# A position matrix added on TensorE, an earlier row maximum, expert choice on logits, and beta added once

## What is computed

```python
prod2 = lhs2 @ rhs2                                  # per batch: 256 x 256, inner size 16
S = softmax(V_s @ sigmoid(prod2 + b_s), axis=1)      # b_s: the position matrix, 256 x 256
out = sum over k of (cheb[k] * S).T @ x, times Theta[k]
y = relu(rw @ x + conv(relu(out)) + biases)
x = x + (y - mean(y)) / sqrt(var(y) + 1e-5) * gamma + beta     # over the 16 times
xn = groupnorm(x)
probs = softmax(xn_tokens @ gate_w.T); rw, sel = top_k(probs, 2); rw = rw / rw.sum()
x = x + sum over the two chosen experts of rw * expert(xn_token)
```

## Time and profile before

| | us |
|---|---|
| median of 3 runs (lowest, highest) | 695.96 (695.71, 696.68) |
| the profiled execution, its own time | 695.89 |
| its span in the trace | 694.1 |
| PE busy over the span | 556.2 (80%) |
| DVE busy | 402.7 (58%) |
| ACT busy | 242.3 (35%) |
| POOL busy | 217.3 (31%) |
| mean granted clock of PE | 0.904 of full |

### The profile page before, as it was taken

How to read it: one execution, slowest core, us unless ns; L and a number is a source line. 1 busy time by engine, 2 the same in 40 slices (tenths; PEclk the granted TensorE clock), 3 DMA queues, 4 the chain that set the end, 5 groups by cost and what they waited for, 6 DMA issues and landing times. The chain is left out here.

```text
span 694.1 us, 11673 instructions
## 1 busy us (share of the span) xinstructions
PE 556.2 (80%) x2488; PEld 363.4 (52%) x2489; DVE 402.7 (58%) x1793; ACT 242.3 (35%) x603; POOL 217.3 (31%) x283
## 2 busy tenths in 40 slices
PE   0567599999999999999982408999999999998243
PEld 0233357766666666766661203666666666665122
DVE  4645226788888888888898552333333333332355
ACT  0343144344444444444431201333333333333232
POOL 5000001224444444444455430344334333434000
PEclk9989599999999999999996556999999999999555
DMA  9900000000000000000000142222222222220796
GB/s 306 415 3 1 1 0 1 0 1 32 31 32 32 31 31 32 32 30 32 32 31 31 49 105 56 90 85 83 81 89 86 83 83 90 89 84 28 219 300 207
DMA packets 36259, 52.84 MB, mean 76 GB/s; under 512 B 4605, under 2 KB 31360, under 8 KB 35968
## 3 DMA queue, kind: packets, MB, share of 16 engines
q1 hardware_dynamic: 24816, 30.86, 14.2%
q0 software_dynamic: 6480, 16.85, 6.6%
q10 hardware_dynamic: 4928, 4.72, 2.1%
HBM read 30.19 MB, written 23.14 MB: 77 GB/s over the span
## 5 line engine op out<-in xcount | busy, mean ns | idle before, releaser
L610 PE MATMUL bank<-w,xT 128*128 x284 | 137.6, 608 | 2.1 <-DVE xT L1399 2.1
L1399 DVE COPY xT<-bank 128x256 f32<-128x256 f32 x71 | 30.2, 425 | 146.9 <-PE bank L597 146.9
L960 POOL DMA_INDIRECT yrows<-xT,dest x71 | 69.4, 977 | 141.4 <-ACT xT L816 135.2
L929 POOL DMA_INDIRECT xrows<-xtok,slot x64 | 67.9, 1061 | 82.1 <-DVEq L1296 67.5
L487 PE MATMUL bank<-work 128*128 128x256 f32 x384 | 93.3, 386 | 0.0
L917 POOL TENSOR_TENSOR yg<-work,sml 128x512 f32<-128x512 f32 x16 | 17.9, 1122 | 187.3 <-DVE work L1206 187.3
L487 PEld LDWEIGHTS bank<-work 128*128 128x128 f32 x384 | 70.4, 190 | 9.0 <-issue 0.8
L625 PE MATMUL bank<-w,xT 128*128 x284 | 73.3, 381 | 1.6 <-ACT xT L821 1.6
L610 PEld LDWEIGHTS bank<-w,xT 128*128 128x128 f32 x284 | 49.3, 194 | 38.2 <-issue 38.2
L810 ACT ACTIVATE xT<-bank 128x256 f32<-128x256 f32 x71 | 27.2, 383 | 98.5 <-PE bank L610 98.5
L625 PEld LDWEIGHTS bank<-w,xT 128*128 128x128 f32 x284 | 48.5, 190 | 6.2 <-issue 2.6
(11 more groups left out here) (201 smaller groups left out, 1020.1 us busy)
## 6 DMA issues: line engine op xcount, KB each, us to landing
xT<-xrows SPq DMA_DIRECT2D x71, 129.0 KB, 2.1
xT<-yrows SPq DMA_DIRECT2D x32, 256.0 KB, 3.9
xs<-x_in SPq DMA_DIRECT2D x4, 1024.0 KB, 11.1
w<-w13t_in SPq DMA_DIRECT2D x1, 4096.0 KB, 18.0
out<-xT ACTq DMA_DIRECT2D x16, 256.0 KB, 3.8
w<-w2t_in SPq DMA_DIRECT2D x1, 2048.0 KB, 22.3
yrows<-xT,dest POOLq DMA_INDIRECT x71, 2.4
xrows<-xtok,slot POOLq DMA_INDIRECT x64, 2.8
```

What stands on the lines that cost most here:

```text
L610: last = mm(bank[2 + q][:, :], xc[:, q, c], w13[:, e, c].rearrange("p w n -> p (w n)"), start=(c == 0), stop=(c == C - 1))
L929: pool.indirect_dma_start(xrows, bass.IndirectOffsetOnAxis(ap=slot[:, q, w, k:k + 1], axis=0), xtok[:, q, k], None).then_inc(sc_done[q], 16)
L960: pool.indirect_dma_start(yrows, bass.IndirectOffsetOnAxis(ap=dest[:, q], axis=0), yo[:, q], None, bounds_check=2 * TOKENS - 1, oob_is_err ...
L1399: V.tensor_copy(xc[:, q].rearrange("p c k -> p (c k)"), bank[q][:, 0:C * P]).then_inc(c_xc, 1)
```

## The change

Six edits, made together:

1. **Position matrix on PE.** Before, DVE added `bs` to the position product and wrote `sg`. Now one product of the identity with `bs`, 512 columns wide, starts PSUM bank 1, the two position products accumulate onto it, and ACT's tanh reads the bank.
2. **Row maximum earlier.** On DVE the softmax part is given to `weave` together with the layer norm's first part, so the row maximum stands right behind the relu of y. ACT takes `exps` ahead of `square`, and tanh ahead of `normalise`.
3. **Choice on logits.** The expert choice compares the logits less their maximum, where it compared softmax probabilities. The first expert has difference 0. ACT takes the exponential of one value per token (2 columns) where it took 16 columns. The two weights 1/(1+e) and e/(1+e) are worked out in `route_c`.
4. **Splits.** `features` uses rows 0 to 63 and 64 to 127 of the array in separate products of 192 columns, into banks 4 and 5. The gate product is split into two token halves of 128 columns that land on partitions 0 and 64. One transpose of 72 rows replaces the two of 8 rows.
5. **Beta once.** POOL no longer adds beta for each batch. ACT adds it to all of `xs` in the prologue, with 16 instructions, one for each time t: 512 elements for each partition, 64 bytes apart, in place. Eight stand ahead of the second group's tanh, four ahead of its exponential, four behind.
6. POOL waits for those 16 ahead of its first turn.

```diff
             def product(b, p):
                 pe.wait_ge(s["b_lr"], done(b))
                 pe.wait_ge(s["b_exp"], done(b - 1))
+                mm(bank[1][:, :], ident, bs[:].rearrange("p c n -> p (c n)"), start=True, stop=False, skip_group_check=True)
                 for c in range(C):
                     last = mm(bank[1][:, c * N:(c + 1) * N], lr[0:T, p, N + c * P:N + (c + 1) * P],
-                              lr[0:T, p, 0:N], start=True, stop=True)
+                              lr[0:T, p, 0:N], start=False, stop=True, skip_group_check=True)
...
             def features(b, p, c):
 
+                pe.wait_ge(s["b_zc"], (b * 4 + c * 2) + START)
                 for h in range(H):
-                    pe.wait_ge(s["b_zc"], (b * 4 + (c * H + h)) + (START - 1))
-                    mm(bank[4 + h][:, 0:K * P], xT[:, b, h, c * P:(c + 1) * P],
-                       thetabd[:].rearrange("p k t o -> p (k t o)"), start=True, stop=True).then_inc(s["b_z"], 1)
+                    for r in range(2):
+                        rows = slice(r * P // 2, (r + 1) * P // 2)
+                        last = mm(bank[4 + r][:, h * K * P // 2:(h + 1) * K * P // 2], xT[rows, b, h, c * P:(c + 1) * P],
+                                  thetabd[rows, :, r * TH // 2:(r + 1) * TH // 2].rearrange("p k t o -> p k (t o)"),
+                                  start=True, stop=True)
...
                 for c in range(C):
-                    last = mm(bank[3][0:E, 0:FT], sm("gate")[:, c * E:(c + 1) * E], xn2[:, c], start=(c == 0),
-                              stop=(c == C - 1))
+                    for k in range(TT):
+                        last = mm(bank[3][64 * k:64 * k + E, 0:P], sm("gate")[:, c * E:(c + 1) * E],
+                                  xn2[:, c, k * P:(k + 1) * P], start=(c == 0), stop=(c == C - 1))
...
+            def add_beta(first, end):
+
+                act.wait_ge(a_xnv, B)
+                act.wait_ge(a_xna, B)
+                for t in range(first, end):
+                    nc.scalar.activation(x_all[:, :, :, t], x_all[:, :, :, t], ACT.Identity,
+                                         bias=sm("beta")[:, t:t + 1], scale=1.0).then_inc(x_beta, 1)
+
...
             normalise_and_copy(1, 6, GB + 2)
+            add_beta(0, T // 2)
             temporal_tanh(1)
+            add_beta(T // 2, 3 * T // 4)
             temporal_exp(1)
+            add_beta(3 * T // 4, T)
...
             def tanh(b, p):
-                act.wait_ge(s["b_bs"], done(b))
-                nc.scalar.activation(sg[:, p], sg[:, p], ACT.Tanh, scale=0.5).then_inc(s["b_th"], 1)
+                act.wait_ge(s["b_pr"], done(b))
+                act.wait_ge(s["b_L"], done(b - 2))
+                nc.scalar.activation(sg[:, p].rearrange("p c n -> p (c n)"), bank[1][:, :], ACT.Tanh, scale=0.5).then_inc(s["b_th"], 1)
...
                 step(nc.gpsimd.tensor_tensor(flat(yg[:]), flat(y[:, p]), over(sm("gamma")), ALU.mult))
-                step(nc.gpsimd.tensor_tensor(flat(yg[:]), flat(yg[:]), over(sm("beta")), ALU.add))
...
-            def add_bs(b, p):
-                dve.wait_ge(s["b_pr"], done(b))
-                dve.wait_ge(s["b_L"], done(b - 2))
-                V.tensor_tensor(sg[:, p].rearrange("p c n -> p (c n)"), bank[1][:, :],
-                                bs[:].rearrange("p c n -> p (c n)"), ALU.add).then_inc(s["b_bs"], 1)
-                yield
-
...
-                weave(centre())
-                weave(router(route_a), statistics())
-                variance = layer_norm()
-                weave(attention(), along=(variance, choice))
-                weave(variance, group_norm(), matrices(), choice)
+                weave(centre(), attention(), router(route_a), statistics())
+                weave(layer_norm(), group_norm(), matrices(), choice)
                 weave(router(route_c))
```

More of the change, by code:

```diff
@@ L534, in turn_logits @@
                 pe.nop(nofuse=True)
-                for k in range(TT):
-                    last = nc.tensor.transpose(bank[3][:, FT + k * E:FT + (k + 1) * E], lgT[0:E, k * P:(k + 1) * P],
-                                               cst[0:E, ID:ID + E])
-                last.then_inc(s["b_lg"], 1)
+                nc.tensor.transpose(bank[3][:, FT:FT + 64 + E], lgT[0:64 + E], cst[0:64 + E, ID:ID + 64 + E]
+                                    ).then_inc(s["b_lg"], 1)
             def prefix(b, p):
@@ L745, in copy_features @@
             def copy_features(b, p, c):
-                for h in range(H):
-                    act.wait_ge(s["b_z"], (b * 4 + (c * H + h + 1)) + START)
-                    nc.scalar.copy(z[:, p, c, :, h], bank[4 + h][:, 0:K * P].rearrange("p (k o) -> p k o", k=K)
+                for r in range(2):
+                    act.wait_ge(s["b_z"], (b * 4 + (c * 2 + r + 1)) + START)
+                    nc.scalar.copy(z[:, p, c, :, :, r * P // 2:(r + 1) * P // 2],
+                                   bank[4 + r][:, 0:K * P].rearrange("p (h k o) -> p k h o", h=H, k=K)
                                    ).then_inc(s["b_zc"], 1)
@@ L977, in _ @@
             V = nc.vector
-            for n in "b_bs b_max b_rec b_A b_y b_cen b_var b_dn b_st b_q b_nb b_sh b_M b_slot".split():
+            for n in "b_max b_rec b_A b_y b_cen b_var b_dn b_st b_q b_nb b_sh b_df b_M b_slot".split():
                 dve.sem_inc(s[n], START)
@@ new lines, in route_b @@
+                step = Steps(dve, v_rt2, b, 10)
+                yield from step.then(V.scalar_tensor_tensor(out=rt[:, 4], in0=rt[:, 0], scalar=0.0, in1=row8(cs(DSC, E)),
+                                                            op0=ALU.is_equal, op1=ALU.mult))
+                yield from step.then(V.tensor_reduce(r2[:, 5], rt[:, 4], AX, ALU.max))
+                yield from step.then(V.tensor_tensor(rt[:, 7], rt[:, 4], wide8(r2[:, 5]), ALU.is_equal))
+                yield from step.then(V.scalar_tensor_tensor(out=rt[:, 5], in0=rt[:, 7], scalar=-3e38, in1=rt[:, 0],
+                                                            op0=ALU.mult, op1=ALU.add))
@@ new lines, in route_b @@
+                yield from step.then(V.tensor_reduce(r2[:, 4], rt[:, 5], AX, ALU.max))
+                dve.sem_inc(s["b_df"], 1)
+                V.tensor_scalar(xtok[:, p, :, N + 1], r2[:, 5], -1.0, float(E), ALU.mult, ALU.add)
+                yield from step.then(V.tensor_tensor(rt[:, 3], rt[:, 5], wide8(r2[:, 4]), ALU.is_equal))
+                yield from step.then(V.tensor_tensor(rt[:, 4], rt[:, 3], row8(cs(DSC, E)), ALU.mult))
+                yield from step.then(V.tensor_reduce(r2[:, 6], rt[:, 4], AX, ALU.max))
@@ L1271, in route_b @@
+                yield from step.then(V.tensor_tensor(rt[:, 8], rt[:, 4], wide8(r2[:, 6]), ALU.is_equal))
                 yield from step.then(V.tensor_tensor(mb[:], rt[:, 7], rt[:, 8], ALU.add))
+                step.close()
                 dve.sem_inc(s["b_M"], 1)
-                V.tensor_scalar(xtok[:, p, :, N + 1], r2[:, 5], -1.0, float(E), ALU.mult, ALU.add)
-                yield from step.then(V.tensor_tensor(r2[:, 7], r2[:, 3], r2[:, 4], ALU.add))
-                yield from step.then(V.reciprocal(r2[:, 8], r2[:, 7]))
@@ L1276, in route_b @@
-                wb = wts[:, b]
-                V.tensor_tensor(wb[:, 0], r2[:, 3], r2[:, 8], ALU.mult)
-                yield from step.then(V.tensor_tensor(wb[:, 1], r2[:, 4], r2[:, 8], ALU.mult))
-                step.close()
             def route_c(b, p):
@@ L1312, in attention @@
                         yield from row_max(i + 1, 1 - q)
-                        yield from pause(2)
+                        yield from pause(3)
                         yield from recip(i + 1, 1 - q)
```

56 lines of the change are left out of this document (23 added, 33 removed).

## The result

The changed kernel is **slower**, by 0.6%: 697.13 us median (691.61 to 701.96, 20 runs) against 693.28 (690.3 to 696.68, 20 runs) for the kernel before in the same measurement. The ratio is 1.0058, 95% interval 1.0038 to 1.0079, so +2.6 to +5.5 us. I had forecast +0.9 us on 695.96.

A forecast was written before the change was run, and what follows sets the result against it. A full turn was taken as bound by a four-piece ring over PE, DVE and ACT. Beta +6.3, filling turns +3.3, full turns -3.5, emptying turns -5.2 gave +0.9 on 695.89: 696.9 us, range 690 to 706.

The forecast's parts named there:

- Full turn: Steady loop turn: four pieces, 7.78, 7.4, 1.18 and 1.20, sum to 17.56 us, 0.3 less; -3.5 over 12 turns.
- c: Prologue: time from one ACT beta instruction to the next, taken as 1.0 us; delay 12c - 5.67, given as +6.3.
- Halves overlap: PE's split products run together, issued in order: 0.9 us for each split of features, 0.55 for the gate product.
- The first rival: Nothing overlaps: halves of features and gate run one after the other, PE decides the turn; +12.7, 709 us; chance 0.18.
- Filling turns: Turns -2 to 1, at the loop's start: PE's added work, mainly the identity product, costs +3.3 us together.
- Turn -1: 0.5: The second filling turn, just before turn 0: the change was to add 0.5 us.
- Emptying turns: Turns 14 to 18, at the loop's end: less work and shorter chains save 5.2 us together.
- The long chain: Turn 18, one dependent chain: fewer choice steps, no exponential wait, split gate and shorter transpose save 2.3 us.
- the ring: Full turn's chain of four pieces over PE, DVE and ACT, from logits to logits; only shortening these shortens the 17.86 us.
- piece (b): DVE's stretch of a full turn, up to ACT's normalisation: 7.01 us before, 7.4 predicted after the change.
- The second rival: Beta's stride in the prologue is nearly free: c of 0.62 takes 4.5 us off, 692 us; chance 0.28.
- The third: Rival: beta's stride costs on source and result sides; c of 1.48, +5.8 us, 703 us; chance 0.12.

The follow-up runs named there:

- e8: Changed kernel with the old order of parts back on DVE and for ACT's exponentials, tanh still ahead of the normalisation; 696.82 us, ratio to before 1.0067.
- e1: Changed kernel, but POOL adds beta to all of xs in 16 instructions ahead of its first turn, ACT none; 693.58 us, ratio to before 1.0021.
- e7: Changed kernel, but POOL adds beta, ten batches ahead of its first turn and one in each of six turns, ACT none; 688.04 us, ratio to before 0.9936.
- f1: e7 plus unused products on PE in its idle stretches; 686.36 us, ratio to before 0.9893.
- f2: The kernel before with the same unused products on PE as f1; 691.05 us, ratio to before 0.9965.
- e6: Changed kernel with unused products on PE in idle stretches of the prologue's end and turns -2 and -1; 690.67 us, ratio to before 0.9983.
- e2: Changed kernel, but POOL adds beta in each turn as in the kernel before, ACT none; 718.09 us, ratio to before 1.039.

## Why the prediction was right or wrong

- **Full turn: right, piece by piece.** 7.78, 7.4, 1.18 and 1.20 were 7.84, 7.36, 1.18 and 1.15; the sum 17.56 was 17.53. PE is not the limit: it idles 0.18 and 0.84 in each turn. I had put its own work at 17.1; it is about 16.4, the length of e8's turn 3, in which it never waits. (12 times 0.3 is 3.6 and not 3.5; it was 3.83.)
- **Beta's price: right.** c = 1.0 was 1.05, so 12c - 5.67 = 6.9 where I had 6.3, and 7.2 at the `mix`. e1 and e7, without it on ACT, start `mix` at 79.0 and 79.2.
- **Halves overlap: right**, and a little better than assumed (0.85 for 0.9; 0.54 for the gate's 0.55, L530 to L535). The first rival is out.
- **Filling turns: the step that failed, +3.3 for +6.05.** To the first `logits` it was +1.08 (I had 1.1), in turn 0 +1.08 and in turn 1 +0.37 (0.86 each); turn -1 was +3.52, and I had 0.5. "Turn -1: 0.5" costed the added work at the clock that turn -1 had before. I left out that this clock is not settled there: in the changed kernel it comes up, falls behind a wait of 2.28 and stays down for 10 us. The runs show +0.65 to +1.35 for the work of all the filling turns when both kernels are warm (f1, f2, e6), less than my 3.3, and 4.7 to 5.4 for the clock. ACT's delay is not needed for the loss (e2, e7); with or without it, four kernels with the change and a short fall of the clock take 3.3 to 4.8 more than the kernel before. Why the fall lasts longer in the changed kernel stays open. This is most of the miss of the sum.
- **Emptying turns: -3.3 for -5.2.** The long chain was right: turns 17 and 18 lose 1.17 and 2.2 (predicted 0.95 and 2.3), turn 16 0.82 (0.6). Turn 14 was wrong. I took 0.7 off for the identity product, but that was never in the ring. What drops out in turn 14 is the position add, which stood in piece (b) of the kernel *before* alone. From `logits` to `prefix` it takes 14.88 (347.02 to 361.90), before 14.26. Turn 15 is 0.28 longer too, not 0.6 shorter, and there it is the clock again: `graph` behind the wait for `prefix` takes 4.51 for its first twelve records, where it took 2.86 before.

```profile
355.77 2.86 PE L487 MATMUL bank<-work 128*128 128x256 f32 x12
```

```profile
364.21 4.51 PE L493 MATMUL bank<-work 128*128 128x256 f32 x12
```

- **The experts don't change: not contradicted.** A single pair of profiles shows -3.67 there, most of it by chance.
- **The second rival** (a nearly free stride) is out by c = 1.05. **The third** too: a stride on both sides did not cost 1.48.

The direction was right mostly by the beta term; the missing clock term and the missing emptying gain raise the loss from +0.9 to the +5.1 of the profiled pair without the late part, and the +4.0 that the ratio gives. That the total still lies beside the forecast is the luck told of above.

## What to carry to other kernels

Where an edit adds work or a longer wait to a stretch in which PE's clock has only just come up, even outside the steady loop, price that stretch at both clocks; one good profile does not tell which of them it will get. Where an edit fills PE's idle time with work, it may gain more than it costs. A one-time job that moves out of the loop still needs a place: put it where its own engine *and* the one that it holds are both idle, and look again at that place once another edit has moved the timeline. Compare stage by stage, and take the stages whose code did not change as the measure of chance.
